# The low parts of the experts' activations on VectorE instead of Pool, in an attention and mixture-of-experts block

## The reference, cut to what matters

```python
xc = x.astype(bfloat16)                     # B, S, 256
normed = (xf * rsqrt(mean(xf*xf) + EPS) * norm_weight).astype(bfloat16)
logits = normed @ gate_weight.T + gate_bias                 # 8 experts
scores, idx = top_k(logits, 2); w = softmax(scores); combine = sum(one_hot(idx, 8) * w[..., None])
p1 = einsum('bsh,eoh->bseo', nf, mlp1_weight) + mlp1_bias   # every expert, 512 outputs
g   = minimum(p1[..., 0::2], 7.0)
lin = clip(p1[..., 1::2], -7.0, 7.0)
act = g * sigmoid(1.702 * g) * (lin + 1.0)                  # 256 per expert
p2 = einsum('bsei,ehi->bseh', act, mlp2_weight) + mlp2_bias
out = xc + einsum('bseh,bse->bsh', p2, combine).astype(bfloat16)
```

## Time and profile before

| what | us |
|---|---|
| median of 3 runs | 1152.02 (1151.81 to 1153.58) |
| the profiled execution, its own time | 1154.16 |
| its span in the profile | 1152.4 |
| PE busy | 965.9 |
| DVE busy | 826.8 |
| ACT busy | 695.2 |
| POOL busy | 424.9 |

### The profile page before, as it was taken

One profiled execution on the slowest core, in us unless ns is written; L12 is line 12 of the kernel. 1 busy time (PEld: TensorE's weight loads), 2 busy tenths in 40 slices (PEclk: granted clock), 3 DMA queues, 4 the chain that ended last, 5 costly groups with the idle time before them and its releaser, 6 DMA issues.

```text
span 1152.4 us, 16694 instructions
## 1 busy us (share of the span) xinstructions
PE 965.9 (84%) x5320; PEld 407.3 (35%) x5320; DVE 826.8 (72%) x1625; ACT 695.2 (60%) x905; POOL 424.9 (37%) x356
## 2 busy tenths in 40 slices
PE   4629997899789997989979997899999998995564
PEld 1312222234343443334433343334443443343243
DVE  4742102589858798588967888587977986897797
ACT  2318885766558574766648665675768777760231
POOL 2413303433444333543354534553332332334243
PEclk9869998999999998999989999999999999998587
DMA  4254444344525253444524345353544453421010
GB/s 157 78 113 79 104 91 96 83 102 111 125 70 134 70 107 101 101 89 114 137 48 110 88 102 125 70 134 83 110 114 98 102 124 94 103 88 38 32 55 32
DMA packets 79971, 109.80 MB, mean 95 GB/s; under 512 B 22522, under 2 KB 56706, under 8 KB 76802
## 3 DMA queue, kind: packets, MB, share of 16 engines
q1 hardware_dynamic: 61444, 83.47, 31.3%
q10 hardware_dynamic: 18432, 25.17, 7.4%
HBM read 82.89 MB, written 25.69 MB: 94 GB/s over the span
## 4 chain that ended last, share of the span: by engine, by line
PE 45%; DVE 26%; issue 9%; DMA 7%; ACT 5%; SPq 4%; POOL 2%; ACTq 1%; DVEq 0%; POOLq 0%
PE OP L692 12%; PE S L678 11%; PE D L664 6%; DVE th_sb L1108 4%; DMA X<-in_x 4%; PE D L569 3%; DVE act_sb L1113 3%; PE A L647 3%; PE D L591 3%; DVE acc L1103 3%; PE BB L647 3%; DVE g_sb L1091 2%; ACT probs L809 2%; DVE l_sb L1093 2%; DVE xn L948 2%
## 5 line engine op out<-in xcount | busy, mean ns | idle before, releaser
L809 ACT ACTIVATE probs<-S 128x1024 f32<-128x1024 f32 x512 | 511.4, 1023 | 209.3 <-PE S L678 208.3
L678 PE MATMUL S<-Qs,Ks 98*128 98x512 bf16 x1024 | 303.6, 389 | 30.7 <-DMA Qs<-m_scr 15.3
L692 PE MATMUL OP<-probs,V 128*17 128x512 f32 x2048 | 275.2, 610 | 2.7 <-ACT O L818 2.7
L893 POOL TENSOR_TENSOR act_lo<-act_sb,act_hi 128x512 fp32r<-128x512 f32 x128 | 166.2, 1299 | 201.9 <-DVE act_hi L1119 163.4
L678 PEld LDWEIGHTS S<-Qs,Ks 98*128 98x128 bf16 x1024 | 80.0, 99 | 213.9 <-ACT probs L809 96.7
L664 PE MATMUL D<-W,act_hi 128*128 128x256 f32 x448 | 130.5, 324 | 22.4 <-DVE acc L1103 12.8
L1103 DVE SCALAR_TENSOR_TENSOR acc<-D,combh,acc 128x256 f32<-128x256 f32 x224 | 97.0, 474 | 51.5 <-PE D L664 51.3
L1108 DVE SCALAR_TENSOR_TENSOR th_sb<-th_sb,g_sb 128x512 f32<-128x512 f32 x128 | 130.4, 1019 | 0.7 <-ACT th_sb L785 0.7
L887 POOL TENSOR_SCALAR W<-W2b 128x512 fp32r<-128x512 bf16 x64 | 47.2, 738 | 212.4 <-PE D L664 207.1
L664 PE MATMUL D<-W,act_lo 128*128 128x256 f32 x448 | 112.5, 283 | 0.0
L785 ACT ACTIVATE th_sb<-g_sb 128x512 f32<-128x512 f32 x128 | 80.1, 626 | 52.2 <-DVE g_sb L1091 50.9
(11 more groups left out here) (136 smaller groups left out, 1038.9 us busy)
## 6 DMA issues: line engine op xcount, KB each, us to landing
W<-in_w ACTq DMA_DIRECT2D x64, 256.0 KB, 2.7
Ks<-k_scr SPq DMA_DIRECT2D x32, 384.0 KB
W2b<-in_w ACTq DMA_DIRECT2D x64, 128.0 KB, 2.8
Ks<-k_scr SPq DMA_DIRECT2D x32, 256.0 KB
o_scr<-O SPq DMA_DIRECT2D x32, 256.0 KB, 4.9
q_scr<-parts SPq DMA_DIRECT2D x16, 384.0 KB, 3.5
k_scr<-parts SPq DMA_DIRECT2D x16, 384.0 KB, 2.6
Qs<-q_scr SPq DMA_DIRECT2D x32, 192.0 KB
```

Of the source, the lines that this page charges most:

```text
L678: last = mm(S[:, j2, C * i:C * (i + 1)], Ks[0:SROWS + MROWS, g % 2, j, P * kt:P * (kt + 1)], Qs[0:SROWS + MROWS, g % 2, j, :], start=True, ...
L692: last = mm(OP[32 * j:32 * j + VW, :], V[:, kt, HG * g + j, :], probs[:, s % 2, C * j:C * (j + 1)], start=kt == 0, stop=kt == KT - 1)
L809: nc.scalar.activation(probs[:, s % 2, 2 * C * j2:2 * C * (j2 + 1)], S[:, j2, :], ACT.Exp, scale=SCALE).then_inc(exp_done, 1)
L893: tt(act_lo[:, e % 2, it, :], act_sb[:, a % 2, :], act_hi[:, e % 2, it, :].bitcast(FP32), ALU.subtract).then_inc(lo_s, 1)
```

## The change

The subtraction of the first seven chunks is issued by DVE, at the same place of the tables (`lo`); the last chunk's stays on Pool. Waits are the same two, of the same values.

```diff
--- before.py
+++ after.py
@@ -885,7 +885,7 @@
-                elif st == "lo":
+                elif st == "lo" and alone(u):
                     e, it = divmod(a, 2)
                     if looped(u) or u or e >= 2:
                         pool.wait_ge(m2_mm, NF * u + 2 * (e - 1))
@@ -1028,7 +1028,7 @@
-                elif st in ("up", "hidden", "down"):
+                elif st in ("up", "hidden", "lo", "down"):
                     expert(st, a, u)
@@ -1117,6 +1117,14 @@
                         v.tensor_copy(act_hi[:, e % 2, it, :], act_sb[:, q, :]).then_inc(hi_s, 1)
+
+                if st == "lo" and not alone(u):
+
+                    dve.wait_ge(hi_s, n + 1)
+                    if looped(u) or u or e >= 2:
+                        dve.wait_ge(m2_mm, NF * u + 2 * (e - 1))
+                    v.tensor_tensor(act_lo[:, e % 2, it, :], act_sb[:, q, :], act_hi[:, e % 2, it, :].bitcast(FP32),
+                                    ALU.subtract).then_inc(lo_s, 1)
```

## The result

The changed kernel took 1160.16 us (median of 5 runs, 1158.39 to 1161.25), the kernel before 1153.58 on the same chip (5 runs, 1151.81 to 1156.99): ratio 1.0053 [1.0031, 1.0076], slower by 0.5%. Forecast: 1148.7. The profiled execution of the changed kernel took 1161.12 us, with a span of 1159.1.

What follows compares the result with a forecast made beforehand. TensorE was taken to bound dense stretches, VectorE the pass starts. Terms -4.4 + 1.5 + 0.5 - 1.75 + 0.8 = -3.35, taken from the median 1152.02, gave 1148.7 us; range 1142.5 to 1157.5.

Steps and rivals of the forecast that it cites:

- Dense stretches, 0: Dense expert steps: TensorE stays the bound, 1.67 us of room against 1.20 added per period, so no change.
- Start of a pass, -1.1 each: Four pass starts: act_sb runs unblocked and X1s starts earlier, so g_sb comes 1.1 us earlier each, -4.4 in sum.
- Before b2, +0.3 each: VectorE's chain to acc before b2, five times: 0.60 comes in, half returned by rope moving earlier; +1.5 in sum.
- rival 1: Slower: other Pool instructions take the lock, 20 act_lo on VectorE's path cost 0.60 each: +12 us, 1164.0; chance 0.13.
- rule for the lock: Shared SBUF port: a two-input VectorE instruction and a Pool instruction reading SBUF take turns; the later is fully blocked.
- the two passes without preparation: Before b2 in two passes preparing no next chunk: th_sb's 0.34 us wait for ACT covers part; +0.26 each, +0.5 together.
- Expert 2, -0.35: Expert 2's halves, five times: Op blocks th_sb instead and act_sb runs free, -0.95 + 0.60 each; -1.75 in sum.
- Tail, +0.8: Seventh chunk's tail, VectorE the path: four act_lo ahead of its last acc cost +0.8 us, upper bound 2.4.
- The third: Clearly faster: shorter idle at pass starts no longer ends in TensorE's low clock, 4 x -2.7 more, 1137.9; chance 0.11.

Runs made afterwards that it cites:

- both kernels filled: Kernel before and changed kernel, each with seven zero products on TensorE ahead of its wait for b2 in five passes: 1145.9 and 1145.4 us.
- lo0_on_pool: Changed kernel with each chunk's first subtraction (7 of 112) back on Pool: 1153.4 us, ratio 0.9999 to the kernel before.
- only_late_on_dve: Kernel before with only the 20 subtractions of half-experts 11 to 15 of the first four chunks on VectorE: 1149.1 us, ratio 0.9965.
- only_middle_on_dve: Kernel before with only the 70 subtractions of half-experts 1 to 10 on VectorE: 1154.9 us, ratio 1.0012.
- only_lo0_on_dve: Kernel before with only the first subtraction of each of seven chunks on VectorE: 1162.2 us, ratio 1.0078.
- only_tail_on_dve: Kernel before with only the tail's five subtractions (half-experts 11 to 15 of the seventh chunk) on VectorE: 1157.0 us, ratio 1.0045.
- late_and_fill_start: Kernel before with 20 late subtractions of the first four chunks on VectorE and twelve zero products ahead of TensorE's wait at four pass starts: 1148.8 us, ratio 0.9961.
- phase_before: Kernel before with four zero products on TensorE behind the product for the logits in five passes: 1154.5 us, ratio 1.0002.
- both_fills: Changed kernel, first subtractions two half steps later, tail's five on Pool, zero products before b2 (seven) and at four pass starts (twelve): 1147.7 us.
- best: Changed kernel, first subtractions two half steps later, tail's five on Pool, seven zero products ahead of the wait for b2 in five passes: 1138.1 us.

## Why the prediction was wrong

Against the kernel before the traces have +9.3 us more in steps 16 to 19 than was forecast (+11.3 against +2.0) and +3.5 more in the tail; the other terms came out as forecast or better.

**Dense stretches, 0: right.** 24.8 and 27.8 us in both kernels, and TensorE was busy for all 24.80.

**Start of a pass, -1.1 each: right, for the stated reason, with one wait that it didn't name.** The timeline of the changed kernel, VectorE, then Pool, then TensorE, as in the earlier trace rows:

```profile
577.20 0.69 DVE L1113 SCALAR_TENSOR_TENSOR act_sb<-l_sb,th_sb 128x512 f32<-128x512 f32 x1
...
578.27 3.69 DVE L948 TENSOR_SCALAR xn<-X,mv,rstd 128x256 f32<-128x256 f32 x4
581.88 0.74 DVE L1091 TENSOR_SCALAR g_sb<-A,b1f 128x512 f32<-128x512 f32 x1
...
578.80 2.37 POOL L873 TENSOR_TENSOR X1s<-X1s,bo_sb 128x1024 f32<-128x1024 f32 x1
...
582.68 0.61 PE L647 MATMUL A<-nfT,W 128*128 128x512 bf16 x2 [3.41 <-DVE g_sb L1091]
```

act_sb runs free, xn takes 3.69 us with X1s over it (forecast near 3.5), and TensorE waits 3.41 us (forecast 3.4 to 4.2). But this wait alone overstates the gain. Ahead of it TensorE waits for acc, and one subtraction now stands in front of acc. The timeline of TensorE in the kernel before and in the changed one:

```profile
575.01 0.39 PE L664 MATMUL D<-W,act_hi 128*128 128x256 f32 x1 [0.59 <-DVE acc L1103]
...
576.62 0.39 PE L664 MATMUL D<-W,act_hi 128*128 128x256 f32 x1 [1.69 <-DVE acc L1103]
```

Over the four passes the waits for g_sb fell by 9.2 us in sum, those for acc rose by 2.4, and g_sb starts 1.3 us earlier from the start of step 4 (1.6, 2.0, 0.8 and 0.8; forecast 1.1 to 1.37). The four stretches lost 6.0 us together, forecast 4.4. The run with these alone gave 4.0, after low clock in steps 16 to 19 took a part back.

**Before b2, +0.3 each: the step that failed.** The timeline of the kernel before, the cast and b2's copy:

```profile
633.42 0.43 DVE L1119 CAST act_hi<-act_sb 128x512 fp32r<-128x512 f32 x1
...
640.79 0.68 DVE L1030 COPY acc<-D 128x512 f32<-128x512 f32 x1
```

And of the changed kernel, VectorE, then Pool, then TensorE, as in the earlier trace rows:

```profile
632.57 0.43 DVE L1119 CAST act_hi<-act_sb 128x512 fp32r<-128x512 f32 x1
...
634.23 0.97 DVE L1126 TENSOR_TENSOR act_lo<-act_sb,act_hi 128x512 fp32r<-128x512 f32 x1
...
637.65 1.65 DVE L1113 SCALAR_TENSOR_TENSOR act_sb<-l_sb,th_sb 128x512 f32<-128x512 f32 x1
639.34 1.37 DVE L1119 CAST act_hi<-act_sb 128x512 fp32r<-128x512 f32 x1
640.63 0.68 DVE L1030 COPY acc<-D 128x512 f32<-128x512 f32 x1
...
633.38 1.27 POOL L861 TENSOR_TENSOR rot<-qb,cos_sb 128x512 f32<-128x512 f32 x1 [6.89 <-ACT qb L755]
636.55 2.20 POOL L863 TENSOR_TENSOR sw<-sw,sin_sb 128x512 f32<-128x512 f32 x1 [1.90 <-DVE sw L955]
...
641.36 2.02 PE L617 MATMUL D<-b2f,combT 8*128 8x256 f32 x4 [1.69 <-DVE acc L1030]
```

Two things were wrong in it. First, the way from cast to copy grew from 7.37 to 8.06 us, +0.7 and not half of 0.6. Half was to come back because rope's multiplications move up. The first did, and then blocked act_lo itself (0.97 us). The second waits for VectorE's shuffle, which now stands behind act_lo: it starts 3.98 us behind the cast, before 3.51. The blocks went from th_sb and act_sb to act_sb and the cast, 2.0 us in sum before and 2.2 after, act_lo's included. This is rival 1's mechanism, at this one place. That the cast, with one input, also blocks (1.37 against 0.43 us) wasn't in the prediction's rule for the lock, which spoke of two inputs, though it had xn, also with one, held by X1s. The Trainium skill (SBUF — State Buffer, "Who interferes with whom") states it: a cast can enter a mode that takes both port pairs. The row agrees as far as the block goes.

Second, and larger: the prediction priced a wait by its length. TensorE's wait even shrank from 1.82 to 1.69 us, where 2.1 was forecast (part of the delay had come at combT, where it now waits 0.79). But behind it the clock stays low for 6.8 us in all five passes, where four of them had 3.4: b2's products take 2.02 us, before 1.13. The prediction had the row that tells of this cost (0.72 from 642 to 648), and used it only against a gain at the pass starts. In steps 16 to 19 the two make +2.3 or +2.4 in four passes and +0.8 in one (it had the long form already), where +1.5 in all was forecast. With the two passes without preparation (+0.5 each, forecast +0.26) it is +11.3, against +2.0. Of this the path is the surer part: 18.4 against 17.7 us with both kernels filled, 0.7 in each of five passes, and the two times 0.5. The other 1.6 us in each of four passes is low clock, which the fill took away. That the first subtraction draws it is not shown: lo0_on_pool, only_late_on_dve and only_middle_on_dve, with nothing new ahead of b2's copy, have 6.8 us in three or four of five passes, and only_lo0_on_dve in no more than three.

**Expert 2, -0.35: right**, -0.3 to -0.4 in each of five passes.

**Tail, +0.8: wrong in size.** Of the changed kernel's timeline, VectorE, then Pool, as in the earlier trace rows:

```profile
1053.03 0.68 DVE L1126 TENSOR_TENSOR act_lo<-act_sb,act_hi 128x512 fp32r<-128x512 f32 x1
...
1054.95 1.04 DVE L1126 TENSOR_TENSOR act_lo<-act_sb,act_hi 128x512 fp32r<-128x512 f32 x1
...
1054.15 1.29 POOL L905 TENSOR_TENSOR Op<-Op,rec_b 128x512 f32<-128x512 f32 x1 [2.78 <-DMA rec_b<-rec_scr]
```

th_sb was rid of its block, as forecast, but Op's multiplication, which waits for a transfer, now blocks act_lo instead. A part of the growth is clock (only_tail_on_dve, 0.78 to 0.73). Adding the five alone cost 5.2 us [3.1, 7.3], against +0.8 and an upper bound of 2.4; taking them back alone gave 2.3, which isn't clear of noise. How much of it is path and how much clock stays open.

**The rivals.** The first came true at two places of its four (b2, +0.7 each, and the tail), and not at the pass starts or at expert 2, where its 0.60 was paid back. The third had the right quantity, the clock, at the wrong place: at the four pass starts low clock did fall, from 23.9 to 17.1 us in sum, but late_and_fill_start shows that it is worth little there. In steps 16 to 19 it rose from 20 to 34 us, and there it counts.

## What to carry to other kernels

Price an operation by the one place where it stands between a wait's releaser and its engine, not by the load of its engine: without 7 of the 112 moved subtractions the loss was gone, and putting them two half steps later took it back as well. Read the waits of one engine in sum: a shorter one can stand behind a longer one. Where TensorE is the path behind a short wait, count also the time at low clock behind it, and consider products with zeros in the wait: seven of them, 1.68 us, gave 0.7% to the kernel before and 1.2% to the one with the first subtraction moved. Check that the filled stretch is TensorE's: at the pass starts, where VectorE is the path, twelve of them gave nothing that can be measured.

## What the hardware showed that was not expected

**Equal waits, unequal clocks.** Within the one execution of lo0_on_pool, TensorE, the fourth and the fifth pass (timeline):

```profile
503.14 1.13 PE L621 MATMUL D<-b2f,combT 8*128 8x256 f32 x4 [1.83 <-DVE acc L1036]
...
634.19 2.07 PE L621 MATMUL D<-b2f,combT 8*128 8x256 f32 x4 [1.83 <-DVE acc L1036]
```

And the stretches of steps 16 to 19 around them:

```profile
493.80:513.00 19.20, 17.14 (x80) 6.04 (x78) 16.09 (x26) 11.52 (x16) 7.60 (x6) 0.91 0.41 96
624.80:645.60 20.80, 18.73 (x80) 6.72 (x78) 16.10 (x24) 11.59 (x16) 7.60 (x6) 0.84 0.38 88
```

The same wait of 1.83 us, the same instructions, and 1.6 us between the stretches: the products behind the wait ran at 2.4 GHz in one, where the clock fell only behind them, for 3.4 us, and at 1.2 in the other, where it stayed low for 6.8. What chooses is open: it isn't the length of the wait, and moving TensorE's work by up to 0.86 us (phase_before) changed it in one pass of five. It makes any edit that shifts TensorE's work worth some us either way: only_middle_on_dve lost at b2 more than it won at expert 2.

**The low clock is worth more than its waits.** Filling 1.7 us of waiting five times, 8.5 us in all, gave 13 to 15 us to the changed kernel.

**TensorE can stand still for 7.4 us without a wait**, in a stretch with all DMA engines full (both_fills, 48 products more than best); the cause was not tried.
